# A transformer block for 32 tiles: the hand-written step order of the fill and the drain made anew on all five engines

## What is computed

```
m = silu(mod) @ w_ada + b_ada                 # 9 shifts, scales and gates per batch
x = x + self_attn(ln(x) * (1 + sc) + sh) * g  # stage A: windows of 128 rows, rolled by 64
x = x + topk_cross_attn(ln(x)*(1+sc)+sh) * g  # stage B: 77 context rows, the 16 best scores kept
x = x + swiglu(ln(x) * (1 + sc) + sh) * g     # stage C: 256 -> 2 x 1024 -> 256
x = x + cross_attn(ada_ln(x, t), ada_ln(ctx, t)) @ Wp + bp   # stage D: 77 context rows
```

## Time and profile before

| | us |
|---|---|
| median of 3 runs | 1008.47 |
| lowest and highest | 1004.64 and 1009.4 |
| the profiled execution's own time | 1009.15 |
| its span | 1007.0 |
| PE busy in the span | 955.5 |
| DVE busy | 851.8 |
| ACT busy | 782.0 |
| POOL busy | 682.3 |

### The profile page before, as it was taken

One profiled execution on the slowest core, in us unless ns is written; L12 is line 12 of the kernel. 1 busy time (PEld: TensorE's weight loads), 2 busy tenths in 40 slices (PEclk: granted clock), 3 DMA queues, 4 the chain that ended last, 5 costly groups with the idle time before them and its releaser, 6 DMA issues.

```text
span 1007.0 us, 32855 instructions
## 1 busy us (share of the span) xinstructions
PE 955.5 (95%) x10750; PEld 836.9 (83%) x10750; DVE 851.8 (85%) x4268; ACT 782.0 (78%) x1679; POOL 682.3 (68%) x1092
## 2 busy tenths in 40 slices
PE   6776899999999999999999999999999999999996
PEld 3564688899988888989898888888999888887784
DVE  1467899999999999999999999999999999889643
ACT  1244678888888888888888888888888888887764
POOL 1158356877777777777777777777777777777763
PEclk9678999999999999999999999999999999999999
DMA  8255400000000000000100011000100100000000
GB/s 281 67 97 89 143 22 7 14 21 23 23 24 23 23 24 13 17 18 23 24 23 23 23 23 23 18 11 19 23 23 23 23 23 18 18 7 7 7 7 16
DMA packets 72153, 33.66 MB, mean 33 GB/s; under 512 B 56520, under 2 KB 68961, under 8 KB 71346
## 3 DMA queue, kind: packets, MB, share of 16 engines
q1 hardware_dynamic: 71986, 31.57, 12.6%
HBM read 22.64 MB, written 8.91 MB: 31 GB/s over the span
## 4 chain that ended last, share of the span: by engine, by line
PE 84%; issue 5%; DVE 4%; POOL 4%; ACT 2%; DMA 0%; DVEq 0%; SPq 0%; POOLq 0%; ACTq 0%
PE ps L2211 22%; PE ps L2222 10%; PE ps L2090 8%; PE ps L2200 8%; PE ps L2176 7%; PE ps L2189 6%; PE ps L2162 4%; PE ps L2138 3%; PE ps L2121 3%; PE ps L2151 3%; PE ps L2101 3%; PE ps L2111 2%; PE ps L2079 2%; PE ps L2011 1%; DVE mx_A L1412 1%
## 5 line engine op out<-in xcount | busy, mean ns | idle before, releaser
L2211 PE MATMUL ps<-hT_C,w_m_sb 128*128 128x128 f32 x2048 | 264.5, 278 | 1.2 <-DVE hidden_C L1555 0.8
L2211 PEld LDWEIGHTS ps<-hT_C,w_m_sb 128*128 128x128 f32 x2048 | 247.4, 192 | 13.7 <-issue 6.8
L934 ACT ACTIVATE silu_C<-ps,cols_sb 128x128 f32<-128x128 f32 x256 | 93.5, 367 | 71.8 <-PE ps L2211 67.7
L2222 PE MATMUL ps<-w_m_sb,hidden_C 128*128 128x256 f32 x512 | 121.1, 379 | 0.0
L601 POOL TENSOR_TENSOR p_B<-p_B,rc_B 128x616 f32<-128x616 f32 x64 | 77.8, 1217 | 51.3 <-DVE p_B L1473 50.7
L1465 DVE MATCH_REPLACE8 scores_left_B<-mx_B,scores_left_B 128x77 f32<-128x77 f32 x512 | 107.7, 223 | 0.0
L1461 DVE MATCH_REPLACE8 scores_left_B<-mx_B,scores_B 128x77 f32<-128x77 f32 x512 | 107.3, 224 | 0.0
L2222 PEld LDWEIGHTS ps<-w_m_sb,hidden_C 128*128 128x128 f32 x512 | 92.4, 190 | 9.9
L1412 DVE TENSOR_REDUCE mx_A<-ps 128x8 f32<-128x1024 f32 x64 | 75.5, 1221 | 22.6 <-PE ps L2121 22.6
L1555 DVE SCALAR_TENSOR_TENSOR hidden_C<-ps,cols_sb,silu_C 128x128 f32<-128x128 f32 x256 | 83.3, 337 | 10.1 <-ACT silu_C L934 9.8
L601 POOL TENSOR_TENSOR p_D<-scores_D,rc_D 128x616 f32<-128x616 f32 x63 | 76.8, 1222 | 16.2 <-DVE rc_D L1510 9.3
(11 more groups left out here) (187 smaller groups left out, 2520.6 us busy)
## 6 DMA issues: line engine op xcount, KB each, us to landing
xn_turned<-xn_blocks_A SPq DMA_DIRECT2D x124, 32.0 KB, 2.0
xn_A<-xn_turned SPq DMA_DIRECT2D x31, 128.0 KB, 2.1
x_A<-in_x SPq DMA_DIRECT2D x28, 128.0 KB, 2.4
out<-y_D SPq DMA_DIRECT2D x28, 128.0 KB, 2.4
w_m_sb<-in_w_m SPq DMA_DIRECT2D x3, 1024.0 KB, 7.9
w_mod_sb<-in_w_mod SPq DMA_DIRECT2D x2, 1024.0 KB, 11.0
gate_b<-row_tables SPq DMA_DIRECT2D x3, 512.0 KB, 5.2
gate<-row_tables SPq DMA_DIRECT2D x2, 512.0 KB, 4.2
```

The costliest lines, as they stand in the source:

```text
L934: sc.activation(SA[:, j, :], bank(f"C.up{j}")[:, 0:P], ACT.Silu, bias=col("bm1_a", j)).then_inc(sa_ok, 1)
L2211: ins = mm(bank(f"C.up{j}")[:, half * P:(half + 1) * P], w_m1[:, k, m:m + P], HT["C"][:, t % HT_COPIES["C"], k, :], start=(k == 0), stop=( ...
L2222: ins = mm(bank("C.dn0")[:, 0:CH], G[:, t % G_COPIES, j, :], w_m2[:, j, :], start=(j == 0), stop=(j == HJ - 1))
```

## The change

Every step, buffer and wait stays as it is; `body(i)` is untouched. In `fill()` and `drain()` of each engine the same steps stand in another order (24 and 10 steps on SP, 84 and 77 on POOL, 172 and 151 on ACT, 172 and 195 on DVE, 184 and 109 on PE). SP's fill is short enough to show whole:

```
             def fill():
                 write_tables()
+                move_input(1)
                 read_tables(0)
-                move_input(1)
+                read_tables(1)
                 load_next_x(2)
+                move_input(2)
+                read_tables(2)
                 load_next_x(3)
                 set_up_flat("B", 0)
+                load_context_weights()
+                load_next_x(4)
                 set_up_flat("B", 1)
-                load_context_weights()
-                move_input(2)
-                read_tables(1)
                 set_up_flat("D", 0)
+                set_up_flat("D", 1)
+                load_next_x(5)
+                move_input(3)
                 load_mlp_weights(0)
-                set_up_flat("D", 1)
-                load_next_x(4)
-                move_input(3)
-                load_next_x(5)
-                load_next_x(6)
                 load_mlp_weights(1)
-                read_tables(2)
                 load_mlp_weights(2)
...
```

In the last iterations the moves are small. Two that the prediction speaks of, on PE and on DVE:

```
                 down(TILES - 1, 0)
+                down(TILES - 1, 1)
                 transpose_p(TILES - 3, "D", 0)
-                down(TILES - 1, 1)
...
                 statistics(TILES - 1, "D")
+                row_sums(TILES - 2, "D")
                 residual(TILES - 3, "D")
-                row_sums(TILES - 2, "D")
```

More of the change, by code:

```diff
@@ L667, in fill @@
[L667 to L676, removed]
+                add_bias(1, "C")
+                less_max(3, "B", 1)
+                divide_a(4)
+                add_bias(3, "B")
@@ L677, in fill @@
+                reciprocal_root(6, "A")
+                reciprocal_root(2, "C")
+                top_less_max(3)
+                less_max(0, "D", 0)
+                reciprocal_root(4, "B")
+                add_bias(2, "C")
+                normalise_weights(3, "B", 0)
+                add_residual(1)
+                add_bias(6, "A")
+                reciprocal_root(1, "D")
+                normalise_weights(3, "B", 1)
+                less_max(0, "D", 1)
                 fold_sums(0)
@@ L1599, in fill @@
-                select(0, 3, 0)
+                select(0, 3, 1)
+                select(0, 1, 1)
+                select(0, 3, 2)
+                select(0, 1, 2)
+                set_up_output_weights(1)
+                select(0, 0, 1)
+                statistics(3, "A")
+                turn_outputs(1)
+                select(0, 0, 2)
+                select(0, 1, 3)
+                turn_back(1)
                 select(0, 2, 0)
-                select(0, 0, 2)
+                residual(1, "A")
@@ L1645, in fill @@
                 row_sums(1, "B")
+                residual(0, "B")
+                select(1, 3, 3)
                 keep_chosen(1, 0)
-                statistics(5, "A")
+                statistics(0, "C")
                 maxima_a(3, 0)
@@ L1700, in fill @@
+                turn_outputs(4)
+                select(3, 0, 1)
                 select(3, 3, 1)
-                turn_outputs(4)
+                select(3, 3, 2)
+                hidden(1, 0)
+                select(3, 0, 2)
+                hidden(1, 1)
                 residual(2, "B")
-                maxima_d(0, 0)
-                hidden(1, 0)
-                hidden(1, 1)
-                statistics(2, "C")
-                select(3, 0, 1)
-                hidden(1, 2)
-                hidden(1, 3)
@@ L1710, in fill @@
-                select(3, 0, 2)
-                maxima_d(0, 1)
-                hidden(1, 4)
-                select(3, 3, 2)
-                turn_back(4)
-                hidden(1, 5)
+                hidden(1, 2)
+                turn_back(4)
+                select(3, 3, 3)
+                hidden(1, 3)
+                statistics(2, "C")
+                hidden(1, 4)
+                select(3, 0, 3)
+                residual(4, "A")
+                hidden(1, 5)
+                statistics(4, "B")
@@ L1834, in drain @@
+                row_sums(TILES - 7, "D")
                 turn_outputs(TILES - 2)
+                turn_input(TILES - 1)
+                select(TILES - 3, 0, 2)
+                turn_back(TILES - 2)
+                residual(TILES - 4, "B")
                 hidden(TILES - 5, 0)
[L1836 to L1837 removed]
                 select(TILES - 3, 3, 1)
+                maxima_d(TILES - 6, 0)
                 hidden(TILES - 5, 1)
                 hidden(TILES - 5, 2)
+                select(TILES - 3, 3, 2)
```

756 lines of the change are left out of this document (366 added, 390 removed).

## The result

| kernel | runs | median us | ratio to before, 95% |
|---|---|---|---|
| before | 20 | 1008.05 | |
| changed | 20 | 1011.09 | 1.0031 (1.0019 to 1.0043) |

The changed kernel is 0.3% slower. The forecast was 1001.2, 0.7% faster, with a range up to 1007.5: wrong in sign.

What follows compares the result with a forecast made beforehand. PE alone was taken to bound the loop from 227 to 896 us, so only its idle time around it could move. Terms of -2.6, -3.0, -1.0, 0 and -0.7 gave -7.3 us: 1001.2 at the median, range 995.5 to 1007.5.

Steps and rivals of the forecast that it cites:

- Term 7: The drain: four matmul rows off the last tile's chain (-0.5 us) and `row_sums(30, "D")` no longer waiting (-0.2), together -0.7.
- Term 1: Start of tile 0: later modulation and gates, a loss of +2.6 us, ends +2.0 and +3.4.
- Terms 2 and 3: Tile 0's `project_o(0)` follows `set_up_values("B")` earlier, -3.9 us; a filled PE gap before 40.17 keeps the clock up, -1.3.
- Term 3: Clock at 40 us: tile 1's keys and queries fill PE's 2.70 us gap, speeding L2050 and L2151; half taken, -1.3 us.
- rival 1: Late transfers: tile 2's x lands some 5 us later, holding DVE; 1007.4 us, no change; chance 0.26 together with Rival 3.
- Terms 4 and 5: The fill from `x_B(0)` through `scores_a(2)` to `scores_t(3)`: gains of -3.0 and -1.0 us.
- Term 4: To `scores_a(2)`: PE's 2.65 us idle before `project_o(1)` goes as `divide_a(1)` moves ahead; tile 2's queries move earlier; -3.0 us.
- Term 5: From `scores_a(2)` to `scores_t(3)`: `add_maxima(2)` first on DVE shortens PE's 3.95 us wait, mostly lost again; -1.0 us.
- Term 6: From `scores_t(3)` to the loop: little PE idle left, DVE's steps only shuffled; 0 us, ends -1.5 and +1.5.
- Rival 3: Gains at the start are given back by the next stage's waits; -4 to 0, 1006.5 us; chance 0.26 together with rival 1.
- Rival 2: Slower: late x(2), late start, lost clock and late `vblk_B` from SP's queue; +3.4 to +7.7 us, 1014; chance 0.07.

## Why the prediction was wrong

The step that failed is in its first part: "What can move is PE's idle time ahead of it and behind it", with the loop from 227 to 896 us counted as fixed. The window is true, but it shows what PE meets, not whose list runs. DVE, POOL and ACT meet their edited drain steps at 847, 868 and 878 us, and 3.0 of the drain's 4.0 us were lost before 907. Term 7 costed only the two moves that were seen at the very end, at -0.7, and put "the same sum of work" at 0; it measured +4.0, shown by the kernel with the old fill and the new drain.

Point by point:
- Term 1 (start, +2.6): right in sign. `scaleT` stood at 9.0 with the old fill and at 9.6 to 10.6 with the new one; the gates' rows came 1.4 us later in the mean (18.1 for 16.8). x(1) landed at 9.0 in the changed kernel's trace, and no later than 10.0 in the others with the new fill; the sum had it at 10.3.
- Terms 2 and 3 (-3.9 and -1.3): larger at their own place, `x_B(0)` 5.0 us earlier in the mean with term 1 in it (44.5 for 49.5), forecast 2.6. Term 3 came at its upper end, 1.8 us on L2050 (3.68 for 5.46) and 0.85 on L2151 (1.08 for 1.93), which the prediction halved. But at `scores_t(1)` 0.9 us were left. In the changed kernel the steps between ran at the slow clock (below). The x of tile 2 was not late: its statistics ran at 38.19, so rival 1 fell.
- Terms 4 and 5 (-4.0): the stretch gave -3.8. The size was luck. Term 4 put PE's 2.65 us before `project_o(1)` down to `divide_a(1)`, though its row names ACT's `qT_A`. That move cost 7.3 us in its trace, and the wait goes where ACT's queries come earlier. Term 5 was read rightly for the old fill (+0.8 us won by its move alone), but in the new fill its stretch gave nothing: from `scores_a(2)` to `scores_t(3)` the means are 33.1 new and 32.8 old. All of the gain lies ahead of `scores_a(2)` (16.4 us from `scores_t(1)`, old 20.5).
- Term 6 (0): +1.5, its upper end, from POOL's and DVE's steps named above.
- Term 7 (-0.7): +4.0, of which +1.0 behind `weigh_values_a(31)`, where its two moves lie. A small reading in it was off as well: four rows of `transpose_p` take 0.66 us (at 926.26 in the changed kernel) and not 0.5.
- The loop: +0.3, not expected.
- Rival 3 (won at the start, given back later) named the right kind of thing, but placed it in the fill and gave it -4 to 0. Rival 2 had the sign (+3.4 to +7.7), by late transfers and late `vblk_B`, and neither came.

The sum of the traces is +1.1 us, the timed difference +3.1 (1.9 to 4.3). A further 1.3 us stand in the changed kernel's trace as the fallen clock near 993 us. Whether that is a property of the new order is not settled: the old drain had a fallen clock there in two of seven traces, and the new drain in one of two.

Why the fifth stretch costs 3.0 us was narrowed to the first part of the drain, on all engines together; no step that was moved explains it, and that is as far as the runs go.

## What to carry to other kernels

In a pipeline in which each engine's list trails another's, find for every engine where its own edited steps begin in time; the loop window of the engine that is the bound doesn't tell. An order of steps on several engines is one object: of fourteen kernels that mixed the two orders or moved single steps, ten were no faster than what they started from, the best of the others gained 1.6 us, and one engine's list taken from the other set cost up to 10. A visible wait of PE tells where an order hurts, not which step to move. Read who ends the wait before naming its cause: a step may wait for a bank that another tile's step must empty, and not for its own input. Then look at what that step stands behind on its engine. The one move in the drain that paid put ready work in front of an engine's own long idle wait.

## What the runs showed of the hardware

**The same code meets the slow clock at different times.** Two kernels with identical lists up to 840 us, windows of 24 to 32 us; first the old fill with the new drain, then the kernel before:

```profile
24.00:32.00 8.00, 5.25 (x49) 3.69 (x53) 3.85 (x8) 0.92 (x2) 1.18 (x4) 1.00 0.36 135
```

```profile
24.00:32.00 8.00, 7.02 (x37) 4.99 (x37) 3.63 (x8) 0.00 (x0) 0.24 (x1) 0.57 0.35 139
```

One ran at 2.4 GHz where the other, by its granted 0.57, spent most of the time at 1.2. `scores_t(7)` stood at 224.84 in the one and 228.20 in the other. So the profiled execution of before, on which the sum was made, had one of the slowest starts of its kernel, and a start can't be judged to better than some 2 us from one trace.

**The filled gap kept the clock up, but not for long.** L2050's first use took 3.68 us in all eight traces in which tile 1's keys and queries stand ahead of `weigh_values_a(0)`, and 4.12 to 5.78 in the ten others; one of the eight is the kernel before with only tile 1 moved early. In the changed kernel PE then went on from 43 to 61 us with 1.4 us of waits (0.34, 0.33 and 0.72), and yet the clock fell during the modulation matmuls (L2011, 4 columns each, from 43.18 on). The rows behind them ran at half speed, L2121 in 2.09 us where the earlier trace rows has 1.15. The granted clock of the two stretches, and a row of the second:

```profile
36.59:41.28 4.69, 4.69 (x48) 3.08 (x48) 2.29 (x7) 1.03 (x3) 1.65 (x5) 1.00 0.10 28
49.61:53.71 4.10, 4.09 (x25) 3.00 (x24) 4.10 (x6) 0.81 (x2) 1.07 (x1) 0.50 0.91 239
```

```profile
49.61 2.09 PE L2121 MATMUL ps<-kblk_A,qT_A 32*128 32x256 f32 x16
```

The new order moved ordinary matmuls into a slow stretch, which took back part of what terms 2 and 3 won.

**DVE and POOL block each other by whole instructions.** L1368 on DVE took 4.36 us for two instructions beside POOL's L502, and 2.34 without; L502 took 6.92 us for four and 4.96. Instruction by instruction (timeline of `divide_a(1)` moved ahead, in narrow windows):

```profile
73.26 1.27 POOL L502 TENSOR_TENSOR vblk_B<-v_flat_sb_B,pair_mask 128x640 f32<-128x640 f32 x1
73.45 2.16 DVE L1368 TENSOR_TENSOR w_out_B<-w_co_sb,gate 128x1024 f32<-128x1024 f32 x1
74.48 2.25 POOL L502 TENSOR_TENSOR vblk_B<-v_flat_sb_B,pair_mask 128x640 f32<-128x640 f32 x1
75.53 2.29 DVE L1368 TENSOR_TENSOR w_out_B<-w_co_sb,gate 128x1024 f32<-128x1024 f32 x1
76.70 2.25 POOL L502 TENSOR_TENSOR vblk_B<-v_flat_sb_B,pair_mask 128x640 f32<-128x640 f32 x1
```

In the kernel before, where the two do not meet, one of these takes 1.21 to 1.22 us on DVE and 1.27 on POOL. POOL's first one, which had started, kept its 1.27. Each of the next four ends 1.08 to 1.13 us after the other engine's instruction ended (74.53, 75.61, 76.73, 77.82, 78.95), so the two took turns by instruction, and the wait is counted in the length of the row. The Trainium skill ("SBUF — State Buffer", Who interferes with whom) says that only the port pair shared by these two engines causes contention, as an exclusive lock. The trace agrees with such a lock: by these lengths (1.21 less 1.08, 1.27 less 1.13) the work of the two overlapped by an estimated 0.15 us at most.
